# Two edits to a vision tower: the order of ScalarE's work in a slot, and the experts' first layer in plain float32, two experts side by side

## The reference

```python
h = layer_norm(x @ fc0_w + fc0_b)                       # 32 channels
for i in range(4):                                      # LAYERS
    h = spectral_conv(h, w1, w2) + einsum(h, conv_w[i]) + conv_b[i]
    h = layer_norm(h); h = gelu(h) if i < 3 else h
h = gelu(h @ fc1_w + fc1_b); h = gelu(h @ fc2_w + fc2_b); h = h @ fc3_w + fc3_b
h = h + attn(layernorm(h))                              # distances of Q and K, softmax(-dist / 8)
xn = layernorm(layernorm(h)) * gamma + beta             # experts: E = 8, D = 64, H = 128, the best 2
y = sum_e w_full[..., e] * (gelu(xn @ W1[e] + b1[e]) @ W2[e] + b2[e])
return h + y
```

## Time and profile before

| | |
|---|---|
| median of 3 runs | 5614.82 us (5611.42 to 5615.45) |
| the profiled execution | 5614.13 us, its span 5612.4 us |
| PE busy | 5147.1 us, 92% |
| VectorE busy | 3916.8 us, 70% |
| ScalarE busy | 3875.5 us, 69% |
| GpSimd busy | 647.3 us, 12% |

### The profile page before, as it was taken

The page is one execution under the profiler, slowest core; times in us unless marked ns, Lnnn a source line. Parts: engine busy times, 40 slices in busy tenths (PEclk is TensorE's granted clock), DMA queues, the critical chain, the costliest instruction groups (busy, mean ns, idle before and its releaser), DMA issues.

```text
span 5612.4 us, 134635 instructions
## 1 busy us (share of the span) xinstructions
PE 5147.1 (92%) x43556; PEld 2927.0 (52%) x43556; DVE 3916.8 (70%) x7712; ACT 3875.5 (69%) x6261; POOL 647.3 (12%) x959
## 2 busy tenths in 40 slices
PE   5878889999999999999999999999999999778778
PEld 2444456666666666666666644433333333334443
DVE  4877888888888888888888865555555554354454
ACT  5888776888666888666888666677777777523333
POOL 0133100233000333000332000000000000000000
PEclk9998899999999999999999999999999999878888
DMA  1334468667687667777676753221111111000000
GB/s 64 129 137 140 138 180 237 225 226 236 213 231 231 226 228 225 232 224 239 222 226 225 229 134 84 57 59 53 53 47 51 53 51 51 8 4 4 7 7 4
DMA packets 398465, 756.32 MB, mean 135 GB/s; under 512 B 246065, under 2 KB 304818, under 8 KB 332602
## 3 DMA queue, kind: packets, MB, share of 16 engines
q1 hardware_dynamic: 378170, 704.04, 39.4%
q0 software_dynamic: 19968, 48.01, 3.8%
HBM read 397.49 MB, written 354.42 MB: 134 GB/s over the span
## 4 chain that ended last, share of the span: by engine, by line
PE 70%; DVE 9%; ACT 8%; issue 7%; SPq 3%; DMA 3%; ACTq 1%; DVEq 0%
PE ps_y L926 10%; PE ps_t L938 8%; PE ps_t L1032 8%; PE ps_t L947 6%; PE ps_f L926 6%; PE ps_y L918 5%; PE ps_f L1017 4%; PE ps_s L903 3%; PE ps_t L1041 2%; PE ps_s L963 2%; DMA big<-hstore 2%; PE ps_t L353 2%; ACT wslot L1211 2%; PE ps_y L892 2%; PE ps_y L1002 2%
## 5 line engine op out<-in xcount | busy, mean ns | idle before, releaser
L1338 DVE TENSOR_REDUCE big<-big 128x16 f32<-128x512 f32 x1280 | 854.0, 675 | 685.3 <-ACT big L1176 681.0
L1331 DVE TENSOR_TENSOR big<-big 128x512 f32<-128x512 f32 x1280 | 938.7, 764 | 30.5 <-DVE big L1360 18.9
L1176 ACT ACTIVATE big<-ps_y 128x512 f32<-128x512 f32 x892 | 545.8, 612 | 482.7 <-PE ps_y L926 425.5
L938 PE MATMUL ps_t<-ident,big 128*128 128x128 f32 x5120 | 809.2, 281 | 55.2 <-DVE big L1331 25.1
L1192 ACT ACTIVATE big<-ps_t,g_now 128x512 f32<-128x512 f32 x1024 | 821.8, 803 | 12.1 <-PE ps_t L938 11.7
L926 PEld LDWEIGHTS ps_y<-conv_now,big 128*128 128x128 f32 x5088 | 616.3, 191 | 362.7 <-issue 362.7
L1185 ACT ACTIVATE big<-ps_t 128x512 f32<-128x512 f32 x1024 | 633.1, 618 | 212.8 <-PE ps_s L963 145.3
L938 PEld LDWEIGHTS ps_t<-ident,big 128*128 128x128 f32 x5120 | 576.1, 143 | 346.8 <-issue 304.6
L947 PE MATMUL ps_t<-ident,big 128*128 128x128 f32 x4096 | 655.5, 283 | 87.1 <-ACT big L1185 84.8
L926 PE MATMUL ps_y<-conv_now,big 128*128 128x128 f32 x5088 | 717.0, 284 | 0.0
L947 PEld LDWEIGHTS ps_t<-ident,big 128*128 128x128 f32 x4096 | 459.4, 143 | 282.0 <-issue 148.9
(11 more groups left out here) (197 smaller groups left out, 7238.6 us busy)
## 6 DMA issues: line engine op xcount, KB each, us to landing
hstore<-big SPq DMA_DIRECT2D x256, 1024.0 KB, 4.1
big<-hstore SPq DMA_DIRECT2D x256, 1024.0 KB, 5.3
xmodes<-x_out SPq DMA_DIRECT2D x128, 312.0 KB, 4.4
y_kt<-ymodes SPq DMA_DIRECT2D x512, 78.0 KB
ymodes<-y_st SPq DMA_DIRECT2D x192, 144.0 KB, 2.5
ymodes<-y_st SPq DMA_DIRECT2D x64, 192.0 KB, 3.3
w_raw<-in_tok_w1r POOLq DMA_DIRECT2D x128, 72.0 KB, 4.5
w_raw<-in_tok_w2r POOLq DMA_DIRECT2D x128, 72.0 KB, 4.4
```

The lines of the kernel that those rows point to most:

```text
L938: last = nc.tensor.transpose(ps_t1[:, 128 * b:128 * b + 128], y_sb[2 * k + wh][:, 128 * b:128 * b + 128], ident[:, :])
L1176: af(y_sq[wh], of[:, wh, :], ACT.Square).then_inc(s["sq_done"], 1)
L1331: v_.tensor_tensor(groups(y_sb[2 * k + wh]), groups(y_sb[2 * k + wh]), rstd[:, k // 2, at:at + 16].unsqueeze(2).to_broadcast([128, 16, 32] ...
L1338: v_.tensor_reduce(ss[:, k // 2, at:at + 16], groups(y_sq[wh]), AX.X, ALU.add).then_inc(s["ss_done"], 1)
```

## The change

In the layer phases ScalarE takes px and the gelu of the second unit ahead of the copy of the first unit's y. The experts' first layer becomes plain float32 of 64 rows: `feat_t` holds the features twice, in rows 0 to 63 and 64 to 127, `w1_pair` the even experts' weights in the upper half and the odd ones' in the lower, and PE issues the first layers of experts t and t + 1 together, on the two halves of the rows, before the even one's turn. The low parts of features and weights go.

```diff
-        feat_t = work(TOK, D)
+        feat_t = work(TOK)
+        w1_pair = work(E // 2 * H).rearrange("p (e h) -> p e h", h=H)
...
                     if t == 0:
-                        pe.wait_ge(a["flow"], i + 1)
-                    wait(pe, a["gw"], i * 2 * E + t - 1)
-                    for part in range(2):
-                        last = mm(ps[t % 2][:, :], w1_hl[:, part, e, :], feat_hl[:, 512 * c:512 * c + 512],
-                                  start=(part == 0), stop=(part == 1))
-                    last.then_inc(a["up"], 1)
+                        pe.wait_ge(a["fcopy"], i + 1)
+                    if t % 2 == 0:
+                        wait(pe, a["gw"], i * 2 * E + t - 1)
+                        wait(pe, a["g"], i * 2 * E + t)
+                        for half in range(2):
+                            r = slice(D * half, D * half + D)
+                            mm(ps[half][:, :], w1_pair[r, e // 2, :], feat_t[r, 512 * c:512 * c + 512], start=True, stop=True
+                               ).then_inc(a["up"], 1)
...
-                af(feat_t, f_flat[0:D, :], ACT.Copy).then_inc(a["feattc"], 1)
-                af(feat_hl[0:D, :], f_flat[0:D, :], ACT.Copy).then_inc(a["fhigh"], 1)
+                af(feat_t[0:D, :], f_flat[0:D, :], ACT.Copy).then_inc(a["feattc"], 1)
+                af(feat_t[D:2 * D, :], f_flat[0:D, :], ACT.Copy).then_inc(a["fcopy"], 1)
...
-                dve.wait_ge(a["fhigh"], it + 1)
-                v_.tensor_tensor(feat_hl[D:128, :], f_flat[0:D, :], feat_hl[0:D, :].bitcast(f32), ALU.subtract
-                                 ).then_inc(a["flow"], 1)
...
-            for r in (slice(0, D), slice(D, 2 * D)):
-                last = v_.tensor_copy(w1_hl[r, 0, :, :], e_w1)
-            last.then_inc(a["split"], 1)
-            dve.wait_ge(a["split"], 2)
-            for r in (slice(0, D), slice(D, 2 * D)):
-                last = v_.tensor_tensor(w1_hl[r, 1, :, :], e_w1, w1_hl[0:D, 0, :, :].bitcast(f32), ALU.subtract)
+            for half in range(2):
+                last = v_.tensor_copy(w1_pair[D * half:D * half + D, :, :],
+                                      e_w1.rearrange("p (e t) h -> p t e h", t=2)[:, half])
...
+                    if front in MIXED and back1 in STORED:
+                        of = y_of(k % 2, True)
+                        px(turned - 2, k, 0, 2 * (n - 1) + k // 2)
+                        if kind in STORED:
+                            gelu(turned, m, kt, 0, kind)
+                        if slots is not None and k == 3:
+                            sign_w2(ph, q - 8, slots[1], 1)
+                        square(unit, 0, of)
+                        px(turned - 1, k, 1, 2 * (n - 1) + k // 2)
+                        if kind in STORED:
+                            gelu(turned + 1, m, kt, 1, kind)
+                        keep_y(unit, k, 0, of)
+                        square(unit + 1, 1, of)
+                        keep_y(unit + 1, k, 1, of)
...
+                        continue
```

More of the change, by code:

```diff
@@ L261, in vit_tower @@
         y_t = keep(TOK, D)
-        feat_hl = z_hl[:, 0, 0, :]
         w_hl = z_hl[0:40, 0, 1, :]
         pick_hl = x_hl[0:40, :, :].rearrange("p a (e h) -> p (a e) h", h=128)
-        w1_hl = z_hl[:, 1, :, :].rearrange("p a (e h) -> p a e h", e=E)
         o_tok = work(512)
@@ L272, in vit_tower @@
             "down", "yc", "yt", "out", "stored", "step", "ones", "qb2",
-            "split", "fhigh", "flow", "wlow")}
+            "split", "fcopy", "wlow")}
         primed += [(a["gw"], 2), (a["down"], 2), (a["out"], 1), (a["yt"], 1), (a["yc"], 1)]
@@ L337, in attention_tensor @@
             pe.wait_ge(a["ones"], 1)
-            pe.wait_ge(a["split"], 3)
+            pe.wait_ge(a["split"], 2)
             def turn(dst, src, rows, width):
@@ L446, in attention @@
                 for n in range(PAIRS):
-                    last = mm(bank_a[:, E * n:E * n + E], feat_t[:, 128 * n:128 * n + 128], r_w, start=True, stop=True)
+                    last = mm(bank_a[:, E * n:E * n + E], feat_t[0:D, 128 * n:128 * n + 128], r_w, start=True, stop=True)
                 last.then_inc(a["logit"], 1)
-                pe.wait_ge(a["flow"], it + 1)
+                pe.wait_ge(a["fcopy"], it + 1)
                 pe.wait_ge(a["w"], it + 1)
@@ L1260, in body @@
                         continue
+                    if front in MIXED and back1 in STORED:
[12 more added lines that the diff above has]
+                        keep_y(unit + 1, k, 1, of)
+                        if slots is not None and k == 1:
+                            sign_w1(ph, q - 8, bass.ds(4 * q - 8 * 4 if slots[0] == 0 else 4 * q - 16 * 4, OCH), slots)
+                            sign_w2(ph, q - 8, slots[0], 0)
+                        continue
                     for wh in range(2):
```

## The result

| | before | after |
|---|---|---|
| median | 5613.22 us (4 runs, 5611.42 to 5615.45) | 5541.95 us (4 runs, 5539.68 to 5542.44) |
| ratio, 95% interval | | 0.9872 [0.9855, 0.9889] |
| profiled execution's span | 5612.4 us | 5540.8 us |

The kernel became 71 us faster, where 44 were forecast. The spans fell by 71.6. Cut by stage, the windows of before give this, with the columns of the earlier trace rows. The rows are the stem, the layers, the head, the first seven iterations, and the last stretch: the eighth iteration with the last 16 experts behind it.

The account below looks back on a forecast made before the run. TensorE's queue was taken to bound the layers, with `turn_out` waiting on the gelu of the unit before. 5614.1 - 44.7 (layers: 30 x 1.25 + 18 x 0.40) + 0.7 (experts' part) = 5570.1 us; range 5548 to 5604.

Parts of the forecast that it names:

- gated slot ends: Layers: three of four slot ends, where `turn_out` waits for gelu1, each 0.40 us shorter, 1.25 a visit.
- the experts' term: Attention and expert stage: the plain float32 first layers by pairs make about +0.7 us, bounds -8 and +11.
- Mixing visits free of DMA: Layers: 30 mixing visits not held by a load of h each gain the whole 1.25 us.
- Of the 1.25 only the 0.40 ahead of that mixing is kept: Layers: 18 mixing visits whose load of h queues behind six loads of modes gain only 0.40 us each.
- Weight visits: Layers, 48 visits where GpSimd adds weights: gain 0, bounds 0.1 us lost and 0.2 won a visit.
- two chains named: Weight visits: slot 2's end set through POOL's addition, then VectorE's slot 3 chain until the forward transform; neither moves.
- Ahead of the loop: Before the attention loop: two VectorE subtractions go, PE then starts on the second load of the tokens, -1.5 us.
- term of +0.55 for a steady iteration: Iterations with experts: first-layer pairs issued ahead lengthen the path by 0.55 us each, times 7 = +3.9.
- rival e: Iterations: PE's clock stays in the bad pattern, 11.7 us more for each of six others, 5640 us; 6%.
- (a): Layers: weight visits gain too, up to 48 x 1.25 us more, 5510 to 5550; 5%.
- (b): Mixing visits: VectorE, keep1 or DMA eat most of the gain, 12 to 25 us left, 5589 to 5602; 12%.
- (d): Experts: a pair's two halves don't overlap, 2.0 instead of 1.07 us a pair, 32 us more, 5602; 3%.

Follow-up runs that it names:

- experiment 1: Kernel before with only ScalarE's new order in the layers and the old experts; 5571.21 us, ratio 0.9937.
- experiment 4: Kernel after with five unread filler matmuls on TensorE in each attention iteration; 5535.95 us, ratio 0.9877.
- experiment 7: Kernel after with SP issuing the modes' loads a visit later, behind the load of h; 5537.28 us, ratio 0.9876.
- experiment 9: Kernel before with ScalarE's new order and GpSimd's addition cut to a small slice; single run 5539.90 us, the 48 weight visits 1164.2 us.
- experiment 2: Kernel before with only the experts' part of the change, ScalarE's old order; 5585.74 us, ratio 0.9960.
- experiment 3: Kernel before with two small memsets on VectorE ahead of the attention loop; 5610.33 us, ratio 1.0008.
- experiment 5: Kernel before, fp32r products kept, with both first layers of a pair of experts issued at the even one; 5599.73 us, ratio 0.9987.
- experiment 8: Kernel before with GpSimd's addition cut to a small slice; single run 5597.55 us, the 48 weight visits 1180.3 us.
- experiment 10: Kernel before with three further gelus ahead of the last 16 experts, so TensorE starts them later; 5591.22 us, one run.
- experiment 11: Experiment 5's kernel with three further gelus ahead of the last 16 experts; 5593.87 us, one run.
- experiment 12: Kernel after with five filler matmuls per iteration and the weight parts' loads at the end of the next visit's SP list; 5500.46 us, ratio 0.9802.
- experiment 6: Kernel before with the experts' plain float32 first layers, each issued singly at its own expert; 5763.76 us, ratio 1.0277.

## Why the prediction was wrong

The direction was right, and so was the price of the gated slot ends; 34 of the 71 us lie in the layers, where 44.7 were forecast. The whole fell outside the range because two terms were wrong, with opposite signs, and because the stem, which had no term, was 10 us shorter too. The larger error is the experts' term: it forecast 0.7 us more and hid a gain of 22.

*Mixing visits free of DMA: right.* 30 visits of after are 38.0 us shorter, 1.27 each, against 1.25. `turn_out` moved as forecast, and nothing else became late.

*"Of the 1.25 only the 0.40 ahead of that mixing is kept": failed.* The 18 visits with a load of h behind the modes (q = 1, 3, 5, 27, 29, 31) are 13.0 us longer than before, +0.72 each, not 0.40 shorter: 20 us off. In experiment 1 it is +10.0 us. The working fixed the issue of the load against the mixing of the visit before, and that held: counted from the start of that visit the load goes out 0.39 us earlier. But the visit before had already been given its whole 1.25, so what it gains behind the mixing was counted twice. Counted from the start of its own visit, the load goes out at 6.6 us where it was 5.7, as a mean of the 18; it takes as long to land as before (8.2 us against 8.1); PE is ready 0.4 us earlier; and its wait grows from 0.6 to 1.9 us. SP's queue of after at such a visit:

```profile
1467.33 2.61 SPq L738 DMA_DIRECT2D ymodes<-y_st  x4
1470.18 6.05 SPq L730 DMA_DIRECT2D mix_room<-xmodes  x6
1476.46 0.63 SPq L702 DMA_DIRECT2D big<-hstore  x1
```

The load of h goes out 9 us after the store of the mixed modes began; it took 7.9 us to land where the median of all 192 is 5.5, and PE waited 2.0 for it. At the same visit of before it took 8.3 us to land, and PE waited 0.4. So the slow landing beside the modes is in both kernels, and what is new is how late it comes for PE.

A second loss stands behind these waits, and the sum has no term for it: the clock. Before's layers run at 2.4 GHz throughout. In after the clock falls to 1.2 GHz in six of the 18 visits, when PE has waited 1.8 to 2.7 us for h, and in none of the others. By the clock's records in the traces the layers have 24 us at 1.2 GHz in after and 20 to 31 in experiments 1, 4, 7 and 9, which have these waits or those for y; before and experiments 2, 3, 5, 8, 10 and 11 have none. One of the six visits of after, whole, and its first products behind the wait:

```profile
1683.99:1713.84 29.85, 27.29 (x296) 20.00 (x289) 22.64 (x45) 18.07 (x32) 0.84 (x2) 0.89 0.88 231
```

```profile
1699.58 1.13 PE L913 MATMUL ps_y<-z_second,c_inh 32*64 32x512 f32 x4 [2.56 <-DMA big<-hstore]
```

The same products take 0.66 us at full clock. These six visits are 2.4 us longer than in before, the other twelve 0.1 us shorter where 0.40 were forecast, so the six hold the whole of the 13.0.

Experiments 7 and 12 confirm the place: with h ahead of the modes the load of y is late, with both ahead of them the 18 visits and six others of odd q fall from 637.3 to 596.0 us, while the 24 of even q, which the loads now stand beside, rise from 601.0 to 612.2.

*Weight visits, "0, with bounds of 0.1 lost and 0.2 won": inside its bounds, at the edge.* 24.39 us against 24.58, 0.19 each and 9.0 over 48, taken as 0. PE wins 0.57 in the second half (from the inverse transform of slot 2 on) and gives 0.38 back in the first. Of the two chains named, VectorE's of slot 3 is the one that holds: the wait of L971 grew from 8.6 to 37.8 us and doesn't move when the addition goes. The chain through POOL was real as a lock and wrong as a bound. By the Trainium skill ("SBUF — State Buffer", on the shared port pair) VectorE's instruction with two inputs in SBUF is blocked while GpSimd's holds the pair. The means of these rows agree, 878 ns against 688; that it kept slot 2's end did not follow, since the time stayed when it was gone. (The prediction's 419 us hold 16 weight visits and parts of mixing visits at either end, not 17. A weight visit of before is 24.58 us by the starts, so its 24.6 stands.)

The layers so: -38.0 + 13.0 - 9.0 = -34.0, against -44.7.

*Ahead of the loop, "-1.5": right.* PE idled 8.51 us before the first iteration in before and 6.76 in after, 1.75 less, and it is the load of the tokens that ends the wait, as forecast. In the head's time (-0.3) it doesn't show, because the same head differs by more than this from profile to profile (in experiment 10, before's program up to there, it took 1617.2 us against 1615.2).

```profile
4822.73 1.97 PE L390 MATMUL ps_s<-ident,big 64*64 64x64 f32 x32 [6.76 <-DMA big<-tok]
```

*The experts, "about +0.7": failed, and this is the larger error.* Their part alone gave 22 us by the ratio. Its single terms were near. A pair of experts at full clock takes 4.05 us against 4.18, so 0.13 less (0.1 to 0.3 a pair was its range). The pairs on the path of a steady iteration, by the chain of waits:

```profile
5163.03 2.01 PE ps_y L364 x4
...
5173.95 1.06 PE ps_y L364 x4
...
5196.58 1.13 PE ps_y L364 x4
```

2.0 and 1.07 were the prices taken from `lift`. A steady iteration is 85.3 us as before, not 85.9, though its granted clock is lower, 0.82 against 0.88. The same 85.3 us stand in nine of the profiles, before, after and experiments 1, 2, 3, 7, 8, 9 and 10, with either first layer. So the term of +0.55 for a steady iteration shows nowhere in its time; why the length stays the same is open.

What the sum lacked is the clock. It treated the granted clock as something that could only go wrong (rival e), and took the last experts as they ran, although 27.3 of their us were at half clock, 27.0 of them with PE never idle; the same experts cost 3.77 us there and 2.09 at full clock. The last stretch lost 9.8 us. In experiment 5's profile issuing two together went with 7.9 of them with the old products, which leaves 1.9 for the plain float32, near the 1.5 of the forecast. How the 7.9 divide between order and moment isn't settled: a later start alone gave 3.9 (experiment 10), and at that later start two together gave 3.2 more (experiment 11). The iterations gave their 17 us all in the first three (261.0 to 243.6 us by their starts), 12.4 of them in the long one (96.6 us, 0.73 granted, against 84.2). It stood in the profiles of before and of experiments 1, 3 and 8 and not in those of 9 and 10, all with the old experts; and in none of the seven with two issued together (after and experiments 2, 4, 5, 7, 11, 12). So it is a matter of the moment that the old order sometimes meets, in 4 of these 6 profiles, and experiment 10 met it not with before's own program. That the new order excludes it is likely and not shown.

*The stem, no term.* Its code is untouched. It took 809.1 us in before's profile with 0.91 granted, and 798.2 to 807.8 in the eleven others whose stem is the same, mostly at 0.92 or above; before's was the longest of them all. Most of these 10 us are then likely a difference between executions and no gain of the change, and they may be part of the spread of before's runs (5588 to 5622). A small part could be the change's: the five stems with ScalarE's new order took 798.2 to 801.8 us, the six others with the old one 798.6 to 807.8. That isn't shown. Where GpSimd's addition is left out the stem took 785.8 and 782.9 us, 12 us below the shortest of the others: in the stem, unlike in the layers, the addition seems to cost time.

*The rivals.* (a) happened in small, 9 us of up to 60. (b), the margins fail, happened for DMA alone. (d) fell: a pair of first layers takes 1.06 to 1.13 at full clock. (e) went the other way among the experts, where the clock was the gain; in the layers the clock cost time, which no rival named.

## What to carry to other kernels

A step on TensorE that has no gap is not yet a step at full speed: read the granted clock of every stretch that is dense, and ask whether the edit changes the order of the products, since a profile with that edit alone had 8 us less in its last stretch and the wrong pairing of type and order cost 150. A wait on a transfer costs more than its length if the clock falls in it. When the wait of a chain is shortened, follow each transfer that is issued from a point inside it to the next visit: its issue may be fixed to the step, its landing isn't, and what the visit before gains behind the issue becomes wait. The fix was the order in SP's queue, 30 us for moving four lines: what is wanted latest goes behind what is wanted next.

## What the runs showed of the hardware

- TensorE stayed at 1.2 GHz for 27.3 us (before), with products without a gap for the last 27.0 of them, and for 78.5 us on end in experiment 6, from 97.3 to 175.8 us of its last stretch, with no gap in the last 66.5. The Trainium skill ("TensorE: Matmul & The Clock Gate", part 1) has the throttle released by activity; these rows have PE's queue full and the clock not given. What the chip counts as activity isn't settled by these runs.
- The same fp32r products in another order, two first layers and then two spreads and second layers, were at half clock for 10.3 and 10.2 us instead of 27.3 and 17.1, the second of each pair with a later start. Short waits of 0.8 to 2.3 us lie in all of these but the 27.3.
- In the layers the clock fell when PE had waited 1.8 to 2.7 us for a load, in 6 of 18 such visits, and the visit took 2.4 us more than before. A wait of 2.7 us was also passed once without it.
- Five products more in an iteration made it 1.3 to 2.0 us shorter, at 0.86 to 0.90 granted against 0.82 in a steady one (experiment 12 against after).
- A VectorE tensor_tensor of 128 x 512 took 688 ns with GpSimd's addition gone and 878 in the mean beside it, without any effect on the end of the weight visits in the old order and with 0.14 us a visit in the new.
